# A local-attention stack: the eight transposes of the queries are placed between the score products

## The reference

```
qkv = x @ Wqkv;  q, k, v = split into 16 heads of 64
q = l2norm(q) * qs;  k = l2norm(k) * ksc          # per head
q = q*cos*scale + rotate_half(q)*sin*scale        # k likewise, with 1/scale
# windows of 32 queries; each sees its own 32 keys and the 32 before
sim = einsum('bhwie,bhwje->bhwij', bq, bk2) * 8, masked
out = softmax(sim) @ v2;   x = out @ Wo + x
x = ffn(shift(x)) + x
```

## Time and profile before

| | value |
|---|---|
| runs | 6353.97, 6337.4, 6340.26 us |
| the profiled execution: its own time, and its span | 6351.3 us, 6349.5 us |
| mean granted clock of TensorE over the span | 0.963 of 2.4 GHz |
| TensorE matmul busy | 90% of the span |
| TensorE weight load busy | 62% |
| VectorE busy | 73% |
| ScalarE busy | 53% |
| GpSimd busy | 68% |

### The profile page before, as it was taken

How to read it: one execution, slowest core, us unless ns; L and a number is a source line. 1 busy time by engine, 2 the same in 40 slices (tenths; PEclk the granted TensorE clock), 3 DMA queues, 4 the chain that set the end, 5 groups by cost and what they waited for, 6 DMA issues and landing times. The chain is left out here.

```text
span 6349.5 us, 177383 instructions
## 1 busy us (share of the span) xinstructions
PE 5684.6 (90%) x76063; PEld 3936.3 (62%) x76063; DVE 4622.9 (73%) x6115; ACT 3391.7 (53%) x4021; POOL 4324.0 (68%) x2122
## 2 busy tenths in 40 slices
PE   7888978898989988889999999999688988889888
PEld 4444447676767776665555655554476776767675
DVE  6455448989989998675556565552588998888896
ACT  1444546666666666434444444434366666666664
POOL 2000048888888888427777777779688888888884
PEclk7889989999999999989999999999799999999999
DMA  0000012222222222100000000000122222222221
GB/s 25 1 2 1 2 45 63 76 63 73 69 68 74 69 70 63 47 1 1 1 1 1 1 1 1 1 1 1 51 63 70 66 76 66 72 67 68 61 69 48
DMA packets 188208, 253.46 MB, mean 40 GB/s; under 512 B 60828, under 2 KB 81816, under 8 KB 187288
## 3 DMA queue, kind: packets, MB, share of 16 engines
q1 hardware_dynamic: 187416, 242.03, 14.7%
HBM read 38.98 MB, written 1.57 MB: 6 GB/s over the span
## 5 line engine op out<-in xcount | busy, mean ns | idle before, releaser
L2092 POOL TENSOR_TENSOR XB<-XB,Pb 128x1024 f32<-128x1024 f32 x448 | 1070.6, 2390 | 338.6 <-ACT Pb L2052 297.5
L906 POOL TENSOR_TENSOR sin_qk<-raw_qk,rot 128x512 f32<-128x512 f32 x768 | 1001.1, 1325 | 11.5 <-ACT raw_qk L868 11.4
L922 POOL TENSOR_TENSOR rot_out<-rot_out,sin_qk 128x1024 f32<-128x1024 f32 x192 | 624.1, 3250 | 412.5 <-DVE rot_out L980 410.8
L2102 DVE TENSOR_REDUCE b_pmax<-slot 128x1 f32<-128x512 f32 x1024 | 653.4, 683 | 324.3 <-PE slot L1839 322.9
L2052 ACT ACTIVATE Pb<-slot 128x1024 f32<-128x1024 f32 x512 | 502.6, 1024 | 702.2 <-PE slot L1950 647.9
L939 POOL TENSOR_TENSOR inv_norm<-norm2c,minus_half 128x16 f32<-128x16 f32 x192 | 682.1, 3553 | 37.2 <-DVE norm2c L1081 23.0
L528 PE MATMUL slot<-w_hi,x_hi 128*128 128x512 f32 x1152 | 556.4, 483 | 120.1 <-DVE rot_out L980 63.4
L931 POOL TENSOR_TENSOR inv_norm<-norm2c,minus_half 128x16 f32<-128x16 f32 x192 | 558.8, 2911 | 55.3 <-DVE norm2c L1028 54.4
L786 ACT ACTIVATE V<-slot 128x1024 f32<-128x1024 f32 x192 | 196.6, 1024 | 598.2 <-PE slot L530 598.2
L1962 PE MATMUL slot<-Pb,Vb 128*64 128x512 f32 x2048 | 496.0, 605 | 1.1 <-ACT Pb L2052 1.1
L984 DVE TENSOR_TENSOR rot_out<-rot_out,inv_norm 128x1024 f32<-128x1024 f32 x384 | 479.5, 1249 | 5.9 <-POOL inv_norm L931 5.2
(11 more groups left out here) (213 smaller groups left out, 13361.7 us busy)
## 6 DMA issues: line engine op xcount, KB each, us to landing
VW<-V SPq DMA_DIRECT2D x1152, 128.0 KB, 2.4
VW<-V SPq DMA_DIRECT2D x768, 64.0 KB, 2.1
w_raw<-in_Wqkv SPq DMA_DIRECT2D x36, 512.0 KB, 3.7
Wo<-in_Wo SPq DMA_DIRECT2D x12, 512.0 KB, 4.4
W<-in_W SPq DMA_DIRECT2D x12, 341.0 KB, 3.2
consts<-in_shape_constants SPq DMA_DIRECT2D x1, 2436.5 KB, 9.2
QH<-rows_dram SPq DMA_DIRECT2D x128, 2.0 KB
QB<-rows_dram SPq DMA_DIRECT2D x128, 2.0 KB
```

The costliest lines, as they stand in the source:

```text
L906: ins = pool.tensor_tensor(dst[:, :, x, :], src[:, :, 1 - x, :], tab, ALU.mult)
L922: pool.tensor_tensor(rot_out[0][:, :], rot_out[0][:, :], rot_sin[0], ALU.add)\
L2092: pool.tensor_tensor(b_sum[:, window % 2, :], Pb[:, (at - 1) % B_RING, :] if k == 1 else b_sum[:, window % 2, :], Pb[:, at % B_RING, :], A ...
L2102: dve.tensor_reduce(b_pmax[:, n // 2, u:u + 1], o[:, 512 * x:512 * x + 512], AX.X, ALU.max)\
```

## The change

The eight transposes of the queries no longer stand together ahead of the scores. The two waits in front of them stay in front, the waits and the two mask matmuls of the scores come next, and then one transpose stands ahead of each two heads' products. The semaphore `tq_mm` is raised by the eighth transpose, which now stands ahead of heads 14 and 15. Where a step has only transposes or only scores (the first and the last chunk of a stack), the other part falls away. No other engine's code changes.

```
-                c = at.chunk(1)
-                if c is not None:
-                    pe.wait_ge(s["qn_done"], START + g + c + 1)
+                q, c = at.chunk(1), at.chunk(2)
+                if q is not None:
+                    pe.wait_ge(s["qn_done"], START + g + q + 1)
                     wait_for_slot2()
-                    turn(slot[2], rot_out[0]).then_inc(s["tq_mm"], 1)
-
-                c = at.chunk(2)
                 if c is not None:
                     pe.wait_ge(s["qT_sb"], START + g + c + 1)
...
-                    for h in range(H):
+                for h in range(H):
+                    if q is not None and h % 2 == 0:
+                        j = h // 2
+                        mm = pe.transpose(slot[2][:, j * 128:(j + 1) * 128], rot_out[0][:, j * 128:(j + 1) * 128], ident)
+                        if j == 7:
+                            mm.then_inc(s["tq_mm"], 1)
+                    if c is not None:
                         r = 64 * (h % 2)
                         col = (h % 2) * 512 + (h // 2) * 64
                         for w in range(4):
...
                                            start=False, stop=True, skip_group_check=True)
+                if c is not None:
                     mm.then_inc(s["s_mm"], 1)
```

## The result

The changed kernel took 6652.32 us (median of four runs, 6648.16 to 6669.41) against 6342.69 us before, a ratio of 1.0491 with a 95% interval of 1.0467 to 1.0515. That is 310 us more; the forecast was 231 us more, 6570 us, with a range of 6440 to 6680. The profiled execution has a span of 6667.6 us and a mean granted clock of 0.949.

What follows compares the result with a forecast made beforehand. The end of the score products was taken to bound most steps. Four steps cost 5.66 us less 1.0 given back; 47.5 fours plus 10 us make 231, so 6340 + 231 = 6571, said as 6570 us, range 6440 to 6680.

Steps and rivals of the forecast that it cites:

- rival 3: The granted clock falls to the 1.2 GHz level in half of the steps: 150 us more, 6720 us; chance 0.10.
- The price of a switch: Between L674 and the value projection: transpose plus two heads' products cost 0.53 us, a chunk 4.84 against 3.02, +1.82 us.
- The slow start that I gave the first mask: At the first mask behind L674: it takes 0.28 us, with the slow start that the first transpose had.
- the bounds, -0.9 and +2.87: Cost per chunk: -0.9 us if transposes run beside other tiles' products, +2.87 if the engine waits out whole records.
- The cover: In the step with tables, one of four, slack leaves about 0.2 of 1.82 us; the three other steps hide nothing.
- What comes back: Stalls ahead of the scores from late code, 0.65 us a chunk: half returns, 0.33 a chunk, 1.0 us per four steps.
- My case of a packet that begins in L674 and ends early in the scores: Such a code packet gains nothing from the spread scores: used up in 3.1 us, against 3.78 from stall to stall.
- The waits: Ahead of the scores, transposes now stand behind the waits; only `XA` was open behind them, 11 times: 10 us more.
- Rival 1: TensorE's waits, some 155 us in both stacks, all shrink and cover more: 6480 us, or 6420 without stalls; chance 0.12.
- Rival 2: Transposes slip between tiles without a switch price, a pair taking 0.24 us; with stalls gone 6220 us; chance 0.05.
- its rule of a break-even at 0.36 us: For transpose-and-products pairs in the scores: from 0.36 us downward, the added 0.63 us a chunk is what the stalls give.

Runs made afterwards that it cites:

- The kernel with one group: Against the kernel before: all eight transposes together, but behind the waits and masks of the scores; 6362.0 us, ratio 1.0009.

## Why the prediction was right, and where its size was off

The direction and the mechanism came as said, and 6652 us lies in the range. But it lies 2 us above the 6490 to 6650 that had the chance of 0.70, in the strip that the range kept for rival 3: the loss was a third more than the sum.

**The price of a switch: right.** Forecast were a pitch of 0.53 us and 4.84 us from the last product of L674 to the value projection; measured 0.53 and, where no stall lies in the stretch, 4.85. In the step shown it is 2126.25 - (2119.95 + 1.48 - 0.22) = 5.04 us, 0.20 of it idle. The shortest stretch before was 3.02, the forecast sum to the digit; the difference is +1.84, forecast +1.82, and in the median +1.77. The slow start that I gave the first mask shows ahead of it and not behind: it starts 0.23 us behind the last product at the least, and the first transpose stands 0.43 behind it. Neither end of the bounds, -0.9 and +2.87, came near.

**The cover: right in kind, its rest under-sized.** The step with tables that is shown kept its length within 0.2 us (17.88 to 18.07). Its slack is used up: the maxima start at 2126.43, 0.1 us behind the end of the last product, where they waited for the tables before, and the key projection at 2128.93, 0.14 us behind the end of the output transposes. In these four steps the other three grew by 5.87 us in sum against the forecast 5.46. But one set of four misleads. Over all clean steps the step with tables grew by 0.64 us in the mean (0.43 in the median; 1.84 - 1.28 of slack would leave 0.56), where 0.2 stood in the sum: 0.2 counted on a stall of 0.39 that the step shown had and most have not. The other three grew by 1.17, 1.26 and 1.66, 1.36 in the mean, where the sum has 1.82 - 0.33 = 1.49.

**What comes back: under-sized.** I took half of the stalls; their idle time before L713 fell by 80 of 102.6 us, more than three quarters. My case of a packet that begins in L674 and ends early in the scores was weighed too heavily. The rule of the Trainium skill (page Runtime: NRT & Kernel Launch, section Instruction fetch mechanics) that the cost of crossing a block of code is mostly hidden holds here only in part: before, 166 of the 384 crossings within the tiled products of L674 and L710 stalled, with over 250 ns between two starts. The stalls ahead of the scores run from 22 to 318 us over kernels that have the same instructions in another order.

**The waits: mis-read, at little cost.** The transposes did not cover 11 waits for `XA` but hid some 28 more that no row showed, because a hidden wait leaves no idle time. The kernel with one group has them all (38 times) and is 0.1% slower, at most 0.2%, with the shorter stalls counted in, so the missing time is not here.

**The clock: the step that failed.** The sum had no term for it; it stood as rival 3 with 0.10. I counted the clock record over the 190 steps. The clean steps took 17.93 us before (169 steps) and 19.11 after (152 steps): +1.18 us, 190 x 1.18 = 225 us, against the forecast 231 (which held 10 for the waits). That this fits so well is in part luck: the steps with tables cost some 31 us where 10 were forecast, the others some 193 where 212 and the 10 were. The rest, 306 - 225 = 81 us, is what the steps that touch the low clock take beyond clean ones: 21 such steps before, 20.13 us each, 46 us in excess, and 38 after, 22.47 us each, 128 in excess. The excess holds the stall that came before the fall as well as the slow work behind it. The granted clock stood at 0.50, the 1.2 GHz level, for 96 us before and 295 us after. What precedes a fall also changed. Before, each of the 21 falls had a gap of at least 1.6 us without a matmul just ahead, 1.8 and more in most cases. After, 14 of the 37 had none over 1.3 us (one 0.42, the others 0.6 to 1.3), a size of gap that stood in the kernel before 146 times and was the longest ahead of none of its falls. Behind a fall it now stayed low for 6.8 or 10.2 us in 34 of 37 cases; before it was 3.4 us in 15 of 21. One such place in the changed kernel:

```profile
1377.10 0.39 PE L713 MATMUL slot<-kT,qT 64*32 64x64 f32 x16
1377.43 0.47 PE L706 MATMUL slot<-consts,rot_out 128*128 128x128 f32 x1
1377.83 0.47 PE L713 MATMUL slot<-kT,qT 64*32 64x64 f32 x16
1378.23 0.47 PE L706 MATMUL slot<-consts,rot_out 128*128 128x128 f32 x1
```

The pitch is 0.80 us in place of 0.53, in the window of clock 0.50 shown at the top. Rival 3 priced a fall in half of the steps at 150 us more; low clock touched a fifth of the steps, a tenth before, and they cost 81 us more.

Is the cause of the clock's part shown? That it fell more often with eight groups is; that the gaps between the small groups do it is a reading that no run shows. The low time was 96 us before, and 106, 73, 147 and 295 with one, two, four and eight groups, each in one profile, so it does not rise with two and rises most with eight. With eight and doubled transposes it was 232: the switches are the same and the array has more work between them, and the excess of the steps with low clock fell from 128 to 112 us while the clean steps grew by 190 x 0.88 = 167. That speaks for the reading, but the total was inside the range of the theory without a clock. The excess per microsecond of low clock was 0.48 us before and 0.43 after. No run removed the clock's part alone; its cause stays open.

Rival 1 (more cover) did not come: the wait for the key copy stayed (62 times, 86.7 us before; 65 times, 88.5 after), it moves with the scores. Only the wait for the cosine half shrank, from 63.4 us (47 times) to 18.0 (25), which is the cover in the step with tables. Rival 2 (no price) is refuted by the pitch, and its rule of a break-even at 0.36 us stands untested.

## What to carry to other kernels

Count the changes between whole-array matmuls and tiled ones before moving a TensorE instruction: here a lone whole-array matmul of 0.11 us between tiled ones cost some 0.26 us more than that, while splitting the same group at a place where such a change stands anyway was free. A wait that something hides leaves no row, so moving work from before a wait to behind it can uncover more waits than the profile lists. Price a change at both clock levels when it breaks a dense stretch of TensorE into small pieces: here a quarter of the loss (81 of 306 us) lay in steps that touched 1.2 GHz. And average over many steps before reading a cost off four of them.

## What the runs showed of the hardware that was not expected

- Every large stall in the tiled products of the kernel before stands at an instruction whose number in TensorE's stream is the same modulo 256 (within one), in 166 of 166 gaps over 250 ns between two starts; the same number holds in the changed kernel and in every experiment. One packet of the instruction queue is 16,384 bytes and took a median of 1.09 us; from its start to the end of the stall passed 2.45 us in the median.
- The same products stalled for 22, 103, 135, 199 and 318 us in sum in five orders of the same instructions. So the cost of late code here went by how dense the instructions are, not by how many.
- The first 32 products behind a change from whole array to tile start about 0.008 us apart (0.24 us from the first to the 32nd), later ones about 0.011 (1.03 us for the other 96), so short groups win back some of their switch. With four groups of 32 products the shortest stretch from mask to value projection was 3.38 us, where 3.6 was expected.
- The clock stayed at 1.2 GHz for 3.4 us in 15 of 21 falls before, and for 6.8 or 10.2 us in 34 of 37 in the changed kernel.
